# The second attention's start moved into the end of the first attention and beside its own first unit

## The chip, the cores and the metric

The kernel runs on one core of a Trainium2 chip. The metric is the device time in microseconds (us) of one execution of the whole program. Five engines work side by side, each in its own program order: TensorE (PE, matrix products and transposes), VectorE (DVE), ScalarE (ACT), GpSimd (POOL) and SyncE (SP, which here only issues DMAs). They wait for one another through semaphores.

## The reference, cut to what matters

One decoder layer in float32 on x of shape (4, 512, 256), in three stages, each followed by `x = layernorm(x + stage(x))`:

```
attention 1:  16 heads of 64, bias by relative position, softmax, output product
attention 2:  q, k, v = x @ Wq, x @ Wk, x @ Wv          (16 heads of 16, causal)
              qc = x @ Wcq;  kc, vc = ctx @ Wck, ctx @ Wcv (no mask)
              y = softmax(q k) v + softmax(qc kc) vc;  y @ Wp + bp
experts:      router picks 3 of 8 per batch; x + sum w_e * gelu(x @ Wa[e]) @ Wb[e]
```

`ctx` has shape (4, 512, 128). The layer norm after attention 1 works on each token's 256 values, so each of the four batches can be normed by itself.

## The kernel before

`x_acc` keeps x in SBUF (16 tiles of 128 tokens by 256) through the whole program. Products run on pairs of half-precision numbers (`hi` and `lo`), three matmuls for one product. `xhi` and `xlo` hold x turned, channels on the partitions.

**attention_1** goes through 32 units (8 head pairs in each of 4 batches, `u // PAIRS` is the batch) in a software pipeline of 37 slots `t`, each of four steps `i`. In slot t unit t is projected, unit t-1 has its maxima taken, t-2 and t-3 their scores and exponentials, and t-4 its output product, added to `x_acc` (`project_out` on PE, `weigh` on ACT, `add_out` on DVE and POOL). Batch 0 is complete in `x_acc` after unit 7. SP moves each unit's halves with 12 DMAs; its bias tiles `rtile` (the relative bias for the maxima) and `near` were loaded in the first eight slots by `load_bias` and kept for all 32 units. PE's own weights are split into halves by ACT (`whi`) and then DVE (`wlo`) while the first slots run, those of the output product by `split_wo` in slot 2.

An all-engine barrier follows (L636), and then **attention_2**, which before its pipeline runs a serial prologue: load ctx and the weights `w2`; norm all 16 tiles (`Normalise`: DVE statistics, ACT root, half of the tiles scaled on DVE, half on ACT); turn ctx (L760) and split it into `chi`, `clo`; split `w2` (L923, L996); turn x for all batches (`Transposed`, L104, L110, L120); and compute the values of all batches (L771 into `v`, stored at L930). Then come 16 units (4 head groups in each of 4 batches) on a clock `CLOCK` that begins at -16, 16 ticks to a unit. The engines walk through the same ticks, and each does what its tick lists:

```
CROSS, SELF, MAX, ROWS_AT, SCORE, VALUE, COPY, TURN, ADD = -12, -5, 16, 33, 38, 42, (49, 57), (56, 63), 64
```

So unit 0 has its cross projection at ticks -12 and -11, its self projection at -5 and -4, unit 1 the same 16 ticks later, and unit 0's maxima (`maximum`, L829 on PE, L1023 on DVE) take ticks 16 to 31, one unit after the other from there. A projection goes PE (L771), ACT (`high_cross` L946, `high_self` L938), DVE (`low_cross` L1012, `low_self` L1006), then SP stores the halves and, when units u and, for an even u, u+1's cross half have been stored, loads them back with 8 DMAs (L745 to L751). `maximum(0, 0)` waits for those 8. Exponentials begin at tick 38.

Afterwards come `output_2`, the router and the experts, which the change does not touch.

Of the kernel before, what the change touches and what calls it, by code (L numbers as in the profile page):

```python
# [11 lines left out]
P = 128  # L12
# [113 lines left out]
def attention_1(nc, io, x_acc, xhi, xlo, ident, lines32, lines16, far_lines):  # L126
# [5 lines left out]
    with ExitStack() as ctx:  # L132
# [3 lines left out]
        def bank(n):  # L136
            return ctx.enter_context(nc.psum_tensor(f"a1_{n}", [P, 512], F32))

        sm = semaphores(nc, ctx, "a1", "x0 x1 x2 x3 w0 w1 w2 w3 w4 w5 w6 w7 bias0 bias1 bias2 bias3 bias4 bias5 bias6 bias7 "
                                       "ld_id ld_bias st_pe st_ev st_r st_l st_f wo cst wsa wsb woa wob ones "  # L140
                                       "pe_a act_a act_v dve_a moved0 moved1 moved2 pe_b dve_b pe_rows act_rows pe_s dve_s act_s pool_p act_ps "
                                       "pool_lo pe_sum dve_r pe_o act_o dve_o pe_e0 pe_e1 dve_x act_x pool_x")
# [7 lines left out]
        rtile = sb("rtile", [P, H1, BAND], F16)  # L150
# [26 lines left out]
        turned = Transposed(nc, ctx, "t1", bank_e, x_acc, ident, (xhi, xlo))  # L177

# [9 lines left out]
        def sync(sp):  # L188
            def load_bias(pair):
                h = slice(2 * pair, 2 * pair + 2)  # L190
                sp.dma_start(rtile[:, h, :], bass.AP(lines16.tensor, 2 * pair * LINE, [[1, P], [LINE, 2], [1, BAND]])
                             ).then_inc(sm[f"bias{pair}"], DMA)
                sp.dma_start(near[:, h, :], bass.AP(lines32.tensor, 2 * pair * S + NEAR_AT, [[1, P], [S, 2], [1, REACH]])
                             ).then_inc(sm[f"bias{pair}"], DMA)
# [5 lines left out]
            def load_w(n):  # L200
                k, cut = w_cuts[n]
                sp.dma_start(wst[n], io["qkv_wT"][k * P:(k + 1) * P, cut]).then_inc(sm[f"w{n}"], DMA)
# [22 lines left out]
            load_bias(0)  # L225
            sp.wait_ge(sm["st_f"], DMA)
            for u in range(UNITS):
# [25 lines left out]
        def tensor(pe):  # L253
# [114 lines left out]

            for t in range(SLOTS):
                for i in range(NT):  # L370
# [23 lines left out]
                    if 0 <= u < UNITS:  # L394
                        pv(u, (i + 2) % 4)

        def scalar(act):
            turned.scalar(act, 0, 1)

            def split_w(n):  # L400
                k, cut = w_cuts[n]
                act.wait_ge(sm[f"w{n}"], DMA)
                act.activation(whi[:, k, cut], wst[n], ACT.Copy, scale=WS).then_inc(sm["wsa"], 1)

            def split_wo():
                act.wait_ge(sm["wo"], DMA)
                act.activation(wohi[:, :, :], wost[:, :, :], ACT.Copy, scale=WS).then_inc(sm["woa"], 1)

# [64 lines left out]
            for t in range(SLOTS):  # L473
                for i in range(NT):
# [25 lines left out]
                    if 0 <= t - 4 < UNITS:  # L500
                        weigh(t - 4, i)

        def vector(dve):
# [7 lines left out]
            def split_wo():  # L511
                dve.wait_ge(sm["woa"], 1)
                dve.scalar_tensor_tensor(wolo[:, :, :], wost[:, :, :], WS, wohi[:, :, :], ALU.mult, ALU.subtract
                                         ).then_inc(sm["wob"], 1)

# [12 lines left out]
            def maximum(u, qb):  # L528
                if qb == 0 and u > 1:
                    dve.wait_ge(sm["pe_rows"], u - 1)  # L530
                if qb == 0 and u < PAIRS:
                    dve.wait_ge(sm[f"bias{u}"], 2 * DMA)
# [1043 lines left out]
```

## Time and profile before

| | us |
|---|---|
| median of three runs (the runs) | 1340.9 (1340.89, 1340.9, 1348.62) |
| profiled execution, its own time | 1347.11 |
| its span | 1345.4 |
| PE, DVE, ACT, POOL busy | 1190.8, 913.5, 830.3, 479.5 |
| granted TensorE clock, mean | 0.951 of full |

The span is cut by the barriers: attention 1 fills it up to 556.4, attention 2 and its output product lie from there to 1048, the router to 1079, the experts to the end. Times on the trace are from the span's start. PE counts as busy while matmuls are in flight, even where they stream at the lower clock.

### The profile page before, as it was taken

How to read it: one execution, taken by the hardware profiler on the slowest of the kernel's cores; microseconds unless marked ns; L12 is line 12 of the kernel's file. 1: busy time of each engine (PE TensorE's matmuls, PEld its weight loads, DVE VectorE, ACT ScalarE, POOL GpSimd, SP SyncE). 2: the span in 40 equal slices, each digit the busy share in tenths (PEclk: the TensorE clock that was granted, in tenths of full speed). 3: DMA queues.
4: the chain of work that ended last, by engine and by line, in shares of the span. 5: the costliest groups of instructions: out<-in, count | busy, mean ns of one | idle time of the engine just before them, and what ended most of it. 6: DMA issues, size and time to landing. Idle time of an engine off the chain costs nothing. (4 is left out here: it accounts for less than half of the span.)

```text
span 1345.4 us, 25018 instructions
## 1 busy us (share of the span) xinstructions
PE 1190.8 (89%) x8862; PEld 552.4 (41%) x8862; DVE 913.5 (68%) x2337; ACT 830.3 (62%) x1584; POOL 479.5 (36%) x511
## 2 busy tenths in 40 slices
PE   6699999999999999375888888888888369999998
PEld 2244444444444443261222232232224336666666
DVE  3777777777777777435788887878841755756564
ACT  3466666666666666450577777677773465666663
POOL 0267888877888888420112111111220000000000
PEclk9999999999999999696799999999997679999999
DMA  7544222222222221202121211212100082332100
GB/s 220 156 98 103 54 57 50 49 51 57 54 57 52 49 49 24 89 8 84 46 69 49 68 52 47 68 46 60 44 2 1 2 313 78 127 125 80 64 16 17
DMA packets 75954, 91.98 MB, mean 68 GB/s; under 512 B 12242, under 2 KB 67538, under 8 KB 75798
## 3 DMA queue, kind: packets, MB, share of 16 engines
q1 hardware_dynamic: 74806, 90.25, 23.9%
q8 instruction: 71, 1.16, 0.4%
q14 instruction: 53, 0.43, 0.1%
q0 software_dynamic: 1024, 0.13, 0.1%
HBM read 54.36 MB, written 10.68 MB: 48 GB/s over the span
## 5 line engine op out<-in xcount | busy, mean ns | idle before, releaser
L1023 DVE TENSOR_REDUCE a_mx<-a_m 128x1 f32<-128x512 f32 (+3 forms) x512 | 269.0, 584 | 74.6 <-PE a_m L829 62.8
L960 ACT ACTIVATE a_pt<-a_s 128x512 f32<-128x512 f32 (+3 forms) x512 | 235.5, 515 | 88.4 <-PE a_s L857 85.1
L449 ACT ACTIVATE a_pt<-a_s 128x512 f32<-128x512 f32 x256 | 149.4, 597 | 164.3 <-DVE a_s L544 135.8
L829 PE MATMUL a_m<-a_k,a_q 48*128 48x512 f16 (+3 forms) x512 | 131.0, 362 | 53.9 <-DVE a_mx L1023 44.2
L537 DVE CUSTOM_DVE_ANT_0 a_junk<-a_m,a_rtile 128x512 f16<-128x512 f32 x256 | 167.3, 687 | 2.0 <-issue 2.0
L604 POOL TENSOR_TENSOR a_ps<-a_ps,a_pt 128x512 f32<-128x512 f32 x128 | 159.9, 1272 | 1.4 <-ACT a_pt L449 1.4
L333 PE MATMUL a_o<-a_pt,a_v 128*64 128x512 f32 x512 | 139.0, 621 | 0.1
L829 PEld LDWEIGHTS a_m<-a_k,a_q 48*128 48x128 f16 x512 | 36.2, 94 | 202.1 <-DVE a_mx L1023 160.7
L870 PE MATMUL a_o<-a_pt,a_v 128*17 128x512 f32 (+3 forms) x1024 | 119.1, 538 | 0.0
L544 DVE TENSOR_TENSOR a_s<-a_s,a_near 128x218 f32<-128x218 f32 (+1 forms) x256 | 108.0, 433 | 15.5 <-PE a_s L324 12.9
L857 PE MATMUL a_s<-a_q,a_k 49*128 49x512 f16 (+3 forms) x512 | 114.4, 352 | 3.3 <-ACT a_pt L960 3.1
L1074 POOL TENSOR_SCALAR_AFFINE_SELECT a_pt<-a_pt 128x512 f32<-128x512 f32 x64 | 40.8, 637 | 210.1 <-ACT a_pt L960 210.1
L1377 ACT ACTIVATE ex_h<-ex_up 128x512 f32<-128x512 f32 x96 | 57.4, 598 | 81.9 <-PE ex_up L1334 81.8
L323 PE MATMUL a_s<-a_q,a_k 128*128 128x512 f16 x256 | 98.9, 387 | 7.6 <-ACT a_pt L449 6.2
L616 POOL TENSOR_TENSOR x_acc<-x_acc,a_part 128x256 f32<-128x256 f32 x128 | 93.1, 727 | 35.2 <-DVE x_acc L564 31.4
L1348 PE MATMUL ex_down<-ex_whi,ex_hh 128*128 128x256 f16 x384 | 104.7, 273 | 0.1
L1348 PE MATMUL ex_down<-ex_wlo,ex_hh 128*128 128x256 f16 x384 | 104.7, 273 | 0.0
L1348 PE MATMUL ex_down<-ex_whi,ex_hl 128*128 128x256 f16 x384 | 104.7, 273 | 0.0
L526 DVE TENSOR_TENSOR a_nat<-a_a,a_nat 128x512 f16<-128x512 f32 x64 | 44.3, 692 | 84.2 <-ACT a_nat L424 84.2
L604 POOL TENSOR_TENSOR a_ps<-a_pt 128x512 f32<-128x512 f32 x64 | 80.1, 1273 | 56.3 <-ACT a_pt L449 56.3
L324 PE MATMUL a_s<-a_q,a_k 74*128 74x512 f16 x256 | 97.8, 382 | 0.0
L609 POOL TENSOR_TENSOR a_psh<-a_ps,a_psh 128x512 f16<-128x512 f32 x64 | 72.9, 1160 | 63.3 <-ACT a_psh L455 63.3
(208 smaller groups left out, 2430.8 us busy)
## 6 DMA issues: line engine op xcount, KB each, us to landing
a_q<-a_nat SPq DMA_DIRECT2D x192, 64.0 KB
a_k<-a_nat SPq DMA_DIRECT2D x192, 64.0 KB
ex_raw<-in_Wa SPq DMA_DIRECT2D x12, 1024.0 KB, 4.9
ex_raw<-in_Wb SPq DMA_DIRECT2D x12, 1024.0 KB, 7.1
halves<-a_natc SPq DMA_DIRECT2D x32, 128.0 KB, 2.4
halves<-a_nat SPq DMA_DIRECT2D x16, 256.0 KB, 2.1
a_q<-halves SPq DMA_DIRECT2D x32, 128.0 KB, 2.7
a_k<-halves SPq DMA_DIRECT2D x32, 128.0 KB, 2.8
```

The lines of the kernel that those rows point to most:

```text
L323: pe.matmul(bank_s[h][:, :], k1[c][:, h, ks], q1[c][:, h, ::-1], start=True, stop=False)
L333: mm = pe.matmul(bank_o[h * D1:(h + 1) * D1, :], v[u % 3][:, kb, h * D1:(h + 1) * D1], pt[:, (8 * u + 2 * kb + h) % RING, :], start=kb == ...
L449: act.activation(pt[:, n % RING, ::-1], bank_s[j % 2][:, :], ACT.Exp, scale=SC1 / QS).then_inc(sm["act_s"], 1)
L537: dve.tensor_tensor_reduce(junk[h][:, :], bank_m[h][:, :], rtile[:, u % PAIRS * 2 + h, qb * P:qb * P + S], 1.0, -3e38, ALU.add, ALU.max, m ...
L544: dve.tensor_tensor(bank_s[h][:, first:end], bank_s[h][:, first:end], near[:, u % PAIRS * 2 + h, at:at + end - first], ALU.add).then_inc(s ...
L604: pool.tensor_tensor(ps[h][:, :], pt[:, (8 * u + h) % RING, :] if kb == 1 else ps[h][:, :], pt[:, (8 * u + 2 * kb + h) % RING, :], ALU.add ...
L829: mm[h] = pe.matmul(bank_m[j % 3][:, 0:keys], q[u % 3][o:o + ROW_M, pair, x, qb * P:(qb + 1) * P], k[u % 3][o:o + ROW_M, pair, x, 0:keys], ...
L857: pe.matmul(bank_s[(32 * u + j) % 3][:, first:], k[u % 3][o:o + ROWS, h // 2, x, kb * P:(kb + 1) * P], q[u % 3][o:o + ROWS, h // 2, x, fir ...
L870: mm = pe.matmul(bank_o[h * 2 * D2:h * 2 * D2 + D2 + 1, first:], v[u // GROUPS][:, x * NT + kb, u % GROUPS * G2 + h, :], pt[g % 4][:, h, f ...
L960: act.activation(pt[g % 4][:, h, first:], bank_s[(32 * u + j) % 3][:, first:], ACT.Exp, scale=SC2 / QS).then_inc(sm["act_s"], 1)
L1023: dve.tensor_reduce(mx[u % 2][:, qb, to:to + 1], bank_m[j % 3][:, 0:keys], AX.X, ALU.max).then_inc(sm["dve_b"], 1)
L1348: mm = pe.matmul(down[t][:, :], a[k][:, f, tok], w[k][:, HALF + f * C:HALF + (f + 1) * C], start=i == 0, stop=i == len(steps) - 1)
```

## The change

Three things are moved.

1. The second attention's weights, small constants and context are loaded during the first. `w2` is split in slots 6 and 10 (`split_w2`, 1280 columns each) out of the buffer `wost`, ctx is turned and split in slot 35 (`turn_context`, `high_context`, `low_context`). To make room, `rtile` becomes a ring of three tiles, reloaded for each unit (`load_toeplitz`, 32 loads in place of 8).
2. Batch 0 is normed (statistics in slot 34, the rest in slot 35) and turned (slot 36) inside attention 1.
3. Batches 1 to 3 are normed, turned, and all values computed, at ticks of attention 2's own clock, in the banks of the scores: statistics at ticks -2, 2, 6; turns at 5 and 6, 12 and 13, 18 and 19; values of batch 0 at -11, -10, -5, -4, of batch 1 at 7, 8, 9, 11, of batch 2 at 14 to 17, of batch 3 at 21, 23, 25, 27.

```diff
+class LayerNorm:           # as Normalise, for one batch b (done: how many were normed before)
+    def statistics(self, dve, b, done):   # 4 bn_stats, 4 bn_aggr, + EPS
+    def root(self, act, b, done):         # Sqrt
+    def even(self, dve, b, done):         # reciprocal, shift, 2 tensor_scalar on x_acc
+    def odd(self, act, b, done):          # 2 activations on x_acc
...
 def attention_1
+            def load_toeplitz(u):
+                if u >= 3:
+                    sp.wait_ge(sm["dve_b"], 8 * (u - 3) + 8)
+                sp.dma_start(rtile[:, u % 3, :, :], bass.AP(lines16.tensor, 2 * (u % PAIRS) * LINE, [[1, P], [LINE, 2], [1, BAND]])
+                             ).then_inc(sm[f"rt{u % 3}"], DMA)
...
+                if u + 1 < UNITS:
+                    load_toeplitz(u + 1)
                 if u + 1 < PAIRS:
-                    load_bias(u + 1)
+                    load_near(u + 1)
+                if u == 4:    # tri_q, identm, ident16, b2, then the first half of w2 into wost
...
+                if u == 8:    # second half of w2
...
+                if u == 12:   # ctx
...
         def tensor(pe):
+                    if t == SLOTS - 2:
+                        turn_context(i)
+                    if t == SLOTS - 1 and i < KC:
+                        turn_first(i)
...
         def scalar(act):
+                    if t in (6, 10) and i == 1:
+                        split_w2(t // 10)
+                    if t == SLOTS - 2:
+                        high_context(i)
+                        if i == 0:
+                            norm.root(act, 0, 0)
+                        if i == 1:
+                            norm.odd(act, 0, 0)
+                    if t == SLOTS - 1 and i < KC:
+                        high_first(i)
...
         def vector(dve):
+                    if t in (6, 10) and i == 1:
+                        split_w2(t // 10)
...
+                    if t == SLOTS - 3 and i == NT - 1:
+                        norm.statistics(dve, 0, 0)
+                    if t == SLOTS - 2:
+                        if i == 1:
+                            norm.even(dve, 0, 0)
+                        low_context(i)
+                    if t == SLOTS - 1 and i < KC:
+                        low_first(i)
...
 def attention_2
+        NORM, TURN_X = (None, -2, 2, 6), (None, (5, 6), (12, 13), (18, 19))
+        VALUES = (-11, -10, -5, -4), (7, 8, 9, 11), (14, 15, 16, 17), (21, 23, 25, 27)
...
         def tensor(pe):
-            (ctx turned, all batches turned, all values)
+            def free(n):       # a bank of the ring bank_s: its last tenant read by ACT (and DVE)
+            def turn_x(b, k):
+                n = turn_number(b, k)
+                free(n)
+                norm.ready(pe, b + 1)
+                for t in range(NT):
+                    o = (b * NT + t) * C + k * P
+                    mm = pe.transpose(bank_s[n % 3][:, t * P:(t + 1) * P], x_acc[:, o:o + P], ident[:, :])
+                mm.then_inc(sm["pe_f"], 1)
+            def values(b, i):
+                n = value_number(b, i)
+                free(n)
+                pe.wait_ge(sm["dve_f"], 2 * b)
...
                 for b in range(B):                 # in each tick after maximum and score,
+                    if b > 0 and n in TURN_X[b]:   # before the projections
+                        turn_x(b, TURN_X[b].index(n))
+                    if n in VALUES[b]:
+                        values(b, VALUES[b].index(n))
...
         def scalar(act):
+                for b in range(1, B):              # in each tick ahead of rows, high_self, high_cross
+                    if n == NORM[b] + 1:
+                        norm.root(act, b, b)
+                    if n == NORM[b] + 2:
+                        norm.odd(act, b, b)
+                (high_x and store_values at the ticks of TURN_X and VALUES)
...
         def vector(dve):
+                for b in range(1, B):              # in each tick ahead of low_self, low_cross
+                    if n == NORM[b]:
+                        norm.statistics(dve, b, b)
+                    if n == NORM[b] + 2:
+                        norm.even(dve, b, b)
+                    if n in TURN_X[b]:
+                        low_x(b, TURN_X[b].index(n))
```

## Rows read from the trace of the kernel before

**Rows 1.** The page's 40 equal slices: granted clock of PE in tenths

```profile
PEclk9999999999999999696799999999997679999999
```

**Rows 2.** Windows: length, busy us of each engine (instructions), clock, DMA share, GB/s

```profile
557.00:582.00 25.00, 10.66 (x48) 9.39 (x48) 20.17 (x58) 13.73 (x24) 0.97 (x5) 0.59 0.38 119
582.00:598.60 16.60, 15.88 (x144) 14.02 (x144) 0.00 (x0) 9.53 (x16) 9.23 (x4) 1.00 0.00 1
598.60:617.30 18.70, 5.26 (x23) 1.76 (x25) 3.00 (x4) 2.79 (x5) 0.00 (x0) 0.85 0.34 98
617.30:640.00 22.70, 18.16 (x82) 5.25 (x82) 18.02 (x34) 1.38 (x2) 0.00 (x0) 0.65 0.20 59
```

**Rows 3.** DVE's timeline in attention 1's full slots, a reciprocal per slot (start, us)

```profile
78.30 0.21 DVE L556 RECIPROCAL a_r<-a_e 128x8 f32<-128x8 f32 x1 [0.42 <-PE a_e L348]
...
140.53 0.21 DVE L556 RECIPROCAL a_r<-a_e 128x8 f32<-128x8 f32 x1 [0.42 <-PE a_e L348]
...
342.63 0.21 DVE L556 RECIPROCAL a_r<-a_e 128x8 f32<-128x8 f32 x1 [0.42 <-PE a_e L348]
```

**Rows 4.** Timeline around `split_wo` in slot 2

```profile
53.12 1.91 ACT L407 ACTIVATE a_wohi<-a_wost 128x2048 f16<-128x2048 f32 x1
...
55.07 2.29 DVE L513 SCALAR_TENSOR_TENSOR a_wolo<-a_wost,a_wohi 128x2048 f16<-128x2048 f32 x1 [1.11 <-ACT a_wohi L407]
...
58.50 0.39 PE L323 MATMUL a_s<-a_q,a_k 128*128 128x512 f16 x1 [2.97 <-ACT a_pt L449]
```

**Rows 5.** Timeline of attention 1's last slots

```profile
547.28 0.48 DVE L564 SCALAR_TENSOR_TENSOR x_acc<-a_e,a_r,x_acc 128x256 f32<-128x256 f32 x1 [3.96 <-PE a_e L365]
...
549.43 0.40 PE L365 MATMUL a_e<-a_wohi,a_a 64*128 64x256 f16 x2 [0.35 <-issue]
...
550.26 0.48 DVE L564 SCALAR_TENSOR_TENSOR x_acc<-a_e,a_r,x_acc 128x256 f32<-128x256 f32 x1 [0.93 <-PE a_e L365]
...
551.75 0.48 DVE L564 SCALAR_TENSOR_TENSOR x_acc<-a_e,a_r,x_acc 128x256 f32<-128x256 f32 x1 [1.00 <-PE a_e L365]
```

**Rows 6.** Timeline of attention 2's prologue

```profile
556.41 5.32 DVE L59 BATCH_NORM_STATS2 t_st<-x_acc 128x6 f32<-128x256 f32 x16 [1.21 <-PEq L636]
...
561.66 1.15 DVE L62 BATCH_NORM_AGGREGATE t_mv<-t_st 128x2 f32<-128x6 f32 x16
...
563.16 1.97 PE L760 MATMUL a_m<-ident,a_pt 128*128 128x128 f32 x8 [8.45 <-DMA a_pt<-in_ctx]
...
563.67 2.67 DVE L70 TENSOR_SCALAR x_acc<-x_acc,t_mv,t_rs 128x256 f32<-128x256 f32 x8
563.79 4.04 ACT L78 ACTIVATE x_acc<-x_acc,t_rs 128x256 f32<-128x256 f32 x8 [0.53 <-DVE t_rs L68]
...
577.86 0.60 ACT L110 ACTIVATE xhi<-a_s 128x512 f16<-128x512 f32 x1 [1.89 <-PE a_s L104]
578.15 0.68 DVE L120 TENSOR_TENSOR xlo<-a_a,xhi 128x512 f16<-128x512 f32 x1
```

**Rows 7.** Timeline: ACT's change of tables before the first exponentials

```profile
646.16 1.28 ACT L960 ACT_TABLE_LOAD   x1
...
647.60 2.06 ACT L960 ACTIVATE a_pt<-a_s 128x512 f32<-128x512 f32 x4 [0.16 <-PE a_s L857]
```

**Rows 8.** Timeline from unit 0's self projection to its first maximum

```profile
604.03 0.75 DVE L1006 SCALAR_TENSOR_TENSOR a_nat<-a_a,a_bias,a_nat 128x512 f16<-128x512 f32 x1 [2.28 <-ACT a_nat L938]
...
606.42 0.75 DVE L1012 SCALAR_TENSOR_TENSOR a_natc<-a_a,a_bias,a_natc 128x512 f16<-128x512 f32 x1 [1.64 <-ACT a_natc L946]
...
617.27 0.29 PE L829 MATMUL a_m<-a_k,a_q 48*128 48x128 f16 x2 [8.57 <-DMA a_k<-halves]
```

**Rows 9.** Windows of 4 us, columns as in Rows 2

```profile
612.00:616.00 4.00, 0.00 (x0) 0.00 (x0) 0.00 (x0) 0.00 (x0) 0.00 (x0) 0.50 0.64 184
...
632.00:636.00 4.00, 3.96 (x15) 0.74 (x13) 2.17 (x4) 0.69 (x1) 0.00 (x0) 0.53 0.01 2
```

**Rows 10.** Timeline: DVE behind a projection placed between unit 0's maxima

```profile
623.54 1.29 DVE L1023 TENSOR_REDUCE a_mx<-a_m 128x1 f32<-128x512 f32 x2 [1.27 <-PE a_m L829]
```

More of the change, by code:

```diff
@@ new lines, with __init__ @@
+QK_AT, CQ_AT, CK_AT = 0, KC * GROUPS * P, KC * GROUPS * P + KC * C
+V_AT = CK_AT + C
+W2 = V_AT + (KC + 1) * C
+class Second:
+    def __init__(self, nc, ctx, x_acc):
+        self.norm = LayerNorm(nc, ctx, "n1", x_acc)
+        self.whi, self.wlo, self.tri_q, self.identm, self.ident16, self.chi, self.clo = (
+            ctx.enter_context(nc.sbuf_tensor(f"a2_{n}", shape, F16))
+            for n, shape in (("whi", [P, W2]), ("wlo", [P, W2]), ("tri_q", [P, 2, P]), ("identm", [P, 2, P]),
+                             ("ident16", [P, P]), ("chi", [P, B * S]), ("clo", [P, B * S])))
+        self.braw, self.bias = (ctx.enter_context(nc.sbuf_tensor(f"a2_{n}", [P, 2 * GROUPS], F32)) for n in ("braw", "bias"))
@@ L132, in attention_1 @@
+def attention_1(nc, io, x_acc, xhi, xlo, ident, second, lines32, lines16, far_lines):
     with ExitStack() as ctx:
@@ L177, in attention_1 @@
         turned = Transposed(nc, ctx, "t1", bank_e, x_acc, ident, (xhi, xlo))
+        norm = second.norm
+        W2_CUTS = [slice(i * (W2 // 2), (i + 1) * (W2 // 2)) for i in range(2)]
+        w2_raw = wost[:, :, :].rearrange("p a c -> p (a c)")[:, 0:W2 // 2]
+        craw = wost[:, :, :].rearrange("p a (t c) -> p (a t) c", c=CC)
+        bank_c = [*bank_s, *bank_m]
+        bank_x = [bank_a, bank_s[0]]
         UNITS = PAIRS * B
@@ L367, in project_out, with turn_context, turn_first @@
                             mm.then_inc(sm[f"pe_e{h}"], 1)
+            def turn_context(b):
+                pe.wait_ge(sm["act_s"], 8 * UNITS)
+                pe.wait_ge(sm["dve_b"], 8 * UNITS)
+                pe.wait_ge(sm["ld_ctx"], DMA)
+                for n in range(NT):
+                    mm = pe.transpose(bank_c[b][:, n * P:(n + 1) * P], craw[:, b * NT + n, :], ident[:, :])
+                mm.then_inc(sm["pe_c"], 1)
+            def turn_first(k):
+                norm.ready(pe, 1)
+                pe.wait_ge(sm["act_rows"], 2 * UNITS)
+                pe.wait_ge(sm["dve_c"], 1)
+                for n in range(NT):
+                    mm = pe.transpose(bank_x[k][:, n * P:(n + 1) * P], x_acc[:, n * C + k * P:n * C + (k + 1) * P], ident[:, :])
+                mm.then_inc(sm["pe_x"], 1)
             for t in range(SLOTS):
@@ L530, in maximum @@
                     dve.wait_ge(sm["pe_rows"], u - 1)
-                if qb == 0 and u < PAIRS:
-                    dve.wait_ge(sm[f"bias{u}"], 2 * DMA)
+                if qb == 0:
+                    dve.wait_ge(sm[f"rt{u % 3}"], DMA * (u // 3 + 1))
                 for h in range(2):
@@ L542, in add_bias @@
                 first, end, at = near_columns(kb)
+                if j == 0 and u < PAIRS:
+                    dve.wait_ge(sm[f"near{u % 2}"], DMA * (u // 2 + 1))
                 dve.wait_ge(sm["pe_s"], 8 * u + j + 1)
@@ L672, in attention_2 @@
         bank_a, bank_o = bank("a"), bank("o")
-        flat = [t[:, :, :].rearrange("p a b -> p (a b)") for t in pt]
-        craw = flat[2].rearrange("p (t c) -> p t c", c=CC)
-        raw = [flat[i][:, 0:W2 // 2] for i in range(2)]
-        w_cuts = [slice(i * (W2 // 2), (i + 1) * (W2 // 2)) for i in range(2)]
-        norm = Normalise(nc, ctx, "t2", x_acc)
-        turned = Transposed(nc, ctx, "t2", bank_s + [bank_a], x_acc, ident, (xhi, xlo))
-        bank_v = bank_m + [bank_a]
+        norm = second.norm
         UNITS = GROUPS * B
@@ L977, in scalar @@
                     exponential(u, 2 * i + 1)
+                for b in range(1, B):
[3 more added lines that the diff above has]
+                        norm.odd(act, b, b)
+                for b in range(B):
+                    if b > 0 and n in TURN_X[b]:
+                        high_x(b, TURN_X[b].index(n))
+                    if n in VALUES[b]:
+                        store_values(b, VALUES[b].index(n))
                 u, i = unit_at(n, ROWS_AT)
```

215 lines of the change are left out of this document (128 added, 87 removed).

## The prediction

> **What bounds the kernel now.** I read the page's slices first: PE's granted clock is at its upper level almost everywhere and falls in two places, slices 17 to 20 and 31 to 33 [rows 1]. The chain that ended last is no help for the first of them, since it is followed back only as far as the experts' first load. So I cut the stretch around the first dip into windows [rows 2]. From 557.0 to 582.0 PE works 10.66 of 25.0 us: norm, loads, weight splits, turns. From 582.0 to 598.6 it computes all values, dense and alone (DVE does nothing). From 598.6 to 617.3 it works 5.26 of 18.7: four projections with their hand-overs, the stores, the loads back. So 60.9 us pass from the barrier (DVE's first instruction at 556.41 [rows 6]) to the first maximum at 617.27 [rows 8]; in them only the values need PE. This is what the change attacks. The stretches on both sides are full. In attention 1 a slot takes 15.55 us ((140.53 - 78.30) / 4 and (342.63 - 140.53) / 13 both give it [rows 3]), one behind the other without a gap. In attention 2's first unit DVE is busy 18.02 of 22.7 us and PE 18.16, at a mean clock of 0.65 [rows 2]: what is put there is not free.
>
> **Part 1, the loads in attention 1.** Twenty-four more loads of `rtile` (448 KB each) stand in SP's queue behind the twelve moves of their slot. In the four slots from 78.30, three of which still issue a bias load (and `near` with it), a slot takes the same 15.55 us as in the thirteen after, which issue none [rows 3]. So I take 0 for them. The wait on `dve_b` that each has is for the maxima of two slots back, and is over when SP comes to it. Two `split_w2` stand in ACT's and DVE's order at step 1 of slots 6 and 10. The row nearest to them is `split_wo`: 1.91 us on ACT and then 2.29 on DVE for 2048 columns, after which PE stood still for 2.97 us [rows 4], 1.2 less than the two together. Scaled to 1280 columns the two take 1.2 + 1.4 = 2.6 us; less the same 1.2 of slack PE loses 1.4. Two of them: **2.8 us** (0 if the slack is wider in the full slots, 5.2 if there is none).
>
> **Part 2, the end of attention 1.** Prices: statistics of one batch (5.32 + 1.15) / 4 and a small sum, 1.8; four turns by PE 1.0 (half of 1.97); a half on ACT 0.60 and on DVE 0.68; two tiles scaled on DVE 0.67 and on ACT 1.0 [rows 6]; a change of tables 1.28 [rows 7]. Statistics begin on DVE at 547.76, behind the last add of slot 34 [rows 5], and end at 549.57, so the reciprocal of slot 35 and its output product start 0.45 later, at 549.85. Before, a round of slot 35 (product 0.83, add 0.48, hand-overs) took 1.49 [rows 5]. Now each round has a context turn on PE, a half on ACT, a half on DVE. Round 0: product to 550.7, turn to 551.75, ACT's half to 552.35, tables to 553.6, root to 553.85. ACT's `weigh` of round 1, which before would have begun at once, begins then. DVE waits for the root too, scales (to 555.0) and splits; ACT scales to 556.0. Round 2's product is done by 555.4 but is weighed only at 556.0 to 556.45; round 3's product runs to 557.5, its turn to 558.5, batch 0's two turns to 560.6, and the last half on DVE ends at 562.0. The barrier falls at about 562.35 in place of 556.41: **5.9 us** later (4 to 8: the tables hidden, or everything in a row).
>
> By the Trainium skill ("ScalarE: Activation LUTs", What ACT_TABLE_LOAD costs) a switch takes about 2.66 us with its drain. Here ACT was back 0.16 us after the load's 1.28, and that 0.16 was for PE [rows 7]; by the page the sum below would be 1.2 us poorer. The number of switches is the same before and after.
>
> **Part 3, from the barrier to the first maximum.** At the upper clock a product of 512 columns takes 0.22 us per matmul and the values 16.6 / 144 = 0.11 [rows 2]. PE: cross(0) first half, `values(0,0)` 1.3, cross(0) second half, done at 565.2. ACT stores those values first (0.6) and then does `high_cross`; DVE's half is done at 566.8. The self projection with the other values of batch 0 between runs to 569.1, and DVE's `low_self(0)` ends at 570.65: 8.3 after the barrier. Before, this took 6.2 (598.6 to 604.78 [rows 2, 8]), so the values cost 2.1 there.
>
> Now comes the wait that the change adds. Before, `low_cross(1)` ended at 607.17, 2.4 after `low_self(0)` [rows 8], and SP needs it before it loads unit 0 back. Now DVE has in front of it: statistics(1), even(1), statistics(2), even(2), low_x(1,0), low_x(1,1), statistics(3). By the prices above, with ACT's roots between (0.5 each with hand-overs): 1.8 + 0.3 + 1.15 + 1.8 + 0.3 + 1.15 = 6.5, at 577.1. ACT scales batch 2 until 577.45, then `high_x(1,0)`, then `high_cross(1)`, then `high_x(1,1)` to 579.35; DVE's second low_x ends at 580.1, statistics(3) at 581.9, `low_cross(1)` at **582.65**: 12.0 after `low_self(0)` in place of 2.4. From there to the first maximum nothing changes: 617.27 - 607.17 = 10.1 [rows 8]. First maximum at 592.75. PE meanwhile does values(1), self(1), turns of batch 2 and two of its values, and by its terms is done at 591.6, just in time. So the front takes 30.4 in place of 60.9. With part 2, the first maximum comes **24.5 us** earlier.
>
> **Part 4, unit 0's maxima.** Still to be done between them on PE: two values of 0.65, two turns of 1.0, batch 3's values (1.3, 1.3, 0.65, 0.65); on DVE two low_x. Half a projection (three matmuls of 0.43 at the lower clock) there left DVE idle for 1.27 [rows 10], so the bank ring of three hides little of it; the same half at the upper clock, 0.65, I take as hidden, and of anything longer 0.6. At the upper clock: turns (1.0 and ACT's 0.6 less what DVE has queued, 0.6; then 0.69 of DVE) 2 x 1.3; long values 2 x 0.7; short ones near 0; in all 4.6. The four projection halves there, 1.3 each before, get 0.65 shorter at the upper clock and give back about 2. Net **2.6**. At the lower clock throughout it is 10.7 (long values 2.6 us each, short 1.3).
>
> **The clock.** PE stood idle for 8.57 us up to 617.27 [rows 8] and its clock was at 0.50 in the window 612 to 616; it was 0.53 still in 632 to 636, with PE busy 3.96 of 4 [rows 9]. In the new order PE's first long idle stretches are 571.5 to 574.3 and 576.4 to 580.1; before and after them it is denser than it was. Each of the three places (batch 0's values and projections, 6.5 us of streams; batch 1's and 2's, 8; the first unit) would run part of its time at 1.2 GHz. Price if all of it does: 5 before `low_self(0)`, 4 before the first maximum, 8 in the unit (10.7 less 2.6). I take a quarter of these 17: **4 us**. This share is a choice; its ends are 0 and 17.
>
> **Sum.** 24.5 - 2.8 - 2.6 - 4 = **15 us**. On the profiled execution 1347.1 would become 1332; the median of the runs lies 6 us under it for reasons outside this stretch, and I carry the same difference over: **1326**.
>
> **The rivals.**
> 1. *The fillers and splits are hidden*: the ring and the slack absorb parts 1 and 4, the clock is up. 24.5 - 0 - 0.5 - 0 = 24: 1317. For it: PE idles in front of the maxima for DVE. Against it: rows 4 and 10.
> 2. *The lower clock stays* from the barrier (mean 0.59 from 557 to 582 [rows 2]) through the first unit: 24.5 - 2.8 - 2.6 - 17 = 2: 1339, no change. Against it: in the first dense stretch after that, from 582.0, the clock was 1.00 at once, and the new front has the same values in it. The skill ("TensorE: Matmul & The Clock Gate", What's actually happening) says that the throttled state is the default and activity releases it; by that this rival ends where the values begin.
> 3. *Slower*: the `rtile` stream is not free. It decides from 15 / 24 = 0.63 us per slot; if each load keeps the moves behind it back so that a slot takes 1.5 us more, 36 us are lost in 24 slots and the time is 1341 + 21 = 1362. For it: these loads now go on in slots where SP's next moves follow closely. Against it: the equal slots [rows 3].
> 4. *It doesn't shorten the front as told*: the norms' chain is longer than my 12.0 (each hand-over 0.2 more, roots behind table loads, 3 x 1.28). Gain 15 - 7 = 8: 1333.
>
> **How the numbers follow.** Forecast (gain 10 to 20) 0.55, hidden 0.15, lower clock 0.13, longer chain 0.11, slower 0.06. The range goes from 1316 to 1338, down to rival 1 and up nearly to rival 2. A difference under 1% (13.4 us) can hardly be told from none here. The bound lies at 1327.5, near my number: of the forecast's 0.55 about 0.42 lies beyond it, with rival 1 0.57, and some of the chain's, so 0.6 faster, 0.33 the same, 0.07 slower.
>
> **What would show it.** Slots of 15.55 us in attention 1 except for two that are about 1.4 longer; the second attention's first instruction near 565 on the new trace (562.35 and the 2.8); `low_cross(1)` some 12 us behind `low_self(0)`, with norm instructions between; the first maximum 30 to 34 us after the barrier; a first unit of 25 to 29 us; no row changed behind it. I am wrong if the slots are longer, if the clock's 0.50 reaches through the first unit, or if PE, not the loads back, releases the first maximum by many us.

## The result and the profile after

The changed kernel takes **1323.46 us** (median of four runs, 1322.84 to 1324.3) where the kernel before, run beside it, takes 1341.38 (1340.89 to 1348.62). The ratio is 0.9854, with a 95% interval from 0.982 to 0.9888: 17.9 us between the medians, 1.5% by the ratio. The forecast was 1326 with a range from 1316 to 1338. The profiled execution took 1322.84 with a span of 1321.1.

First the page of the changed kernel, as in [rows 1]: in slices 17 to 20 the granted clock reads 8, 8, 8, 7 in place of 6, 9, 6, 7, and the load of `rtile` is there 32 times.

```profile
PEclk9999999999999999888799999999999689999999
...
a_rtile<-lines SPq DMA_DIRECT2D x32, 448.0 KB, 3.9
```

Next DVE's timeline of the changed kernel in attention 1, as in [rows 3]: a slot takes 15.55 us as before (127.55 to 143.09, 223.00 to 238.55) with a tile loaded in each of them, but 17.71 from 109.84 to 127.55, where the first half of `w2` is split. The second such slot, 174.19 to 191.89, takes 17.70.

```profile
109.84 0.21 DVE L707 RECIPROCAL a_r<-a_e 128x8 f32<-128x8 f32 x1 [0.42 <-PE a_e L441]
127.55 0.21 DVE L707 RECIPROCAL a_r<-a_e 128x8 f32<-128x8 f32 x1 [0.43 <-PE a_e L441]
143.09 0.21 DVE L707 RECIPROCAL a_r<-a_e 128x8 f32<-128x8 f32 x1 [0.42 <-PE a_e L441]
...
223.00 0.21 DVE L707 RECIPROCAL a_r<-a_e 128x8 f32<-128x8 f32 x1 [0.43 <-PE a_e L441]
238.55 0.21 DVE L707 RECIPROCAL a_r<-a_e 128x8 f32<-128x8 f32 x1 [0.42 <-PE a_e L441]
```

The timeline inside that slot (start, length, engine, operation, and in brackets the idle time before it and what ended it), to be held against [rows 4]. ACT works 1.27 us, DVE 1.58, and PE then stands for 1.24 because `a_a` comes from DVE, which was busy with the split. Nine of the profiles of this study have two such slots; sixteen of the eighteen take 17.7 and two take 19.1 and 19.2 (norms later, tail). In these two PE stands for the same 1.24, but the granted clock is down to 0.66 and 0.75 in the 4 us that follow, where the changed kernel has 1.00.

```profile
116.12 1.27 ACT L524 ACTIVATE a_whi<-a_wost 128x1280 f16<-128x1280 f32 x1
...
117.43 1.58 DVE L653 SCALAR_TENSOR_TENSOR a_wlo<-a_wost,a_whi 128x1280 f16<-128x1280 f32 x1 [0.64 <-ACT a_whi L524]
...
119.75 1.08 PE L426 MATMUL a_o<-a_pt,a_v 128*64 128x512 f32 x4 [1.24 <-DVE a_a L700]
```

The timeline of attention 1's end in the changed kernel, as in [rows 5]. The statistics stand in front of slot 35's reciprocal; then the change of tables, the root 0.02 us behind it, the scaling between the adds; the last `xlo`; and attention 2's first instructions, POOL's at 566.22 and PE's at 566.26 (before, DVE's at 556.41 [rows 6]).

```profile
552.72 1.39 DVE L140 BATCH_NORM_STATS2 n_st<-x_acc 128x6 f32<-128x256 f32 x4
...
554.52 0.19 DVE L707 RECIPROCAL a_r<-a_e 128x8 f32<-128x8 f32 x1
...
557.33 1.28 ACT L150 ACT_TABLE_LOAD   x1
...
558.63 0.20 ACT L150 ACTIVATE n_rs<-n_rs 128x4 f32<-128x4 f32 x1
...
565.25 0.68 DVE L663 TENSOR_TENSOR xlo<-a_s,xhi 128x512 f16<-128x512 f32 x1
...
566.22 1.08 POOL L1239 MEMSET a_v<- 128x128 f32 x3 [2.39 <-POOLq L800]
...
566.26 0.38 PE L914 MATMUL a_a<-xhi,a_whi 128*128 128x512 f16 x1 [1.84 <-PEq L800]
```

The timeline of the new front, as in [rows 8]: `low_self(0)`, then three rounds of statistics, and only then `low_cross(1)` at 585.74. SP's first load back is issued at 589.57, and the first maximum is at 597.71 after an idle of 1.50 in place of 8.57.

```profile
573.70 0.75 DVE L1177 SCALAR_TENSOR_TENSOR a_nat<-a_a,a_bias,a_nat 128x512 f16<-128x512 f32 x1 [3.16 <-ACT a_nat L1106]
...
577.45 1.40 DVE L140 BATCH_NORM_STATS2 n_st<-x_acc 128x6 f32<-128x256 f32 x4
...
583.29 1.40 DVE L140 BATCH_NORM_STATS2 n_st<-x_acc 128x6 f32<-128x256 f32 x4
...
585.74 0.74 DVE L1183 SCALAR_TENSOR_TENSOR a_natc<-a_a,a_bias,a_natc 128x512 f16<-128x512 f32 x1
...
589.57 0.61 SPq L901 DMA_DIRECT2D a_q<-halves  x1
...
597.71 0.23 PE L990 MATMUL a_m<-a_k,a_q 48*128 48x128 f16 x2 [1.50 <-DMA a_k<-halves]
```

Windows of the changed kernel, columns as in [rows 2]: barrier to first maximum, the first three units, and the stretch from the last unit's maxima to the router.

```profile
566.20:597.00 30.80, 20.48 (x133) 14.65 (x133) 14.87 (x48) 14.48 (x27) 8.48 (x8) 0.83 0.23 65
...
597.71:620.53 22.82, 19.24 (x138) 9.53 (x138) 19.05 (x36) 6.16 (x10) 2.35 (x1) 0.95 0.21 60
...
620.50:643.10 22.60, 19.72 (x123) 6.25 (x123) 18.45 (x35) 11.43 (x24) 3.75 (x6) 0.65 0.21 59
643.10:668.70 25.60, 23.73 (x190) 7.21 (x192) 18.95 (x39) 17.18 (x37) 3.58 (x6) 0.88 0.18 53
...
971.89:1024.41 52.52, 42.22 (x262) 23.36 (x254) 9.03 (x19) 27.52 (x57) 5.78 (x9) 0.97 0.00 1
```

The last one in the kernel before:

```profile
990.07:1048.60 58.53, 49.05 (x262) 24.01 (x254) 9.03 (x19) 27.74 (x57) 5.78 (x9) 0.83 0.00 1
```

To measure a unit I use DVE's small operation that closes its maxima (the first maximum opens the first). Of these closings the kernel before has, for units 0, 1, 2 and 15,

```profile
640.02 0.18 DVE L1030 TENSOR_SCALAR a_mx<-a_mx 128x32 f16<-128x32 f32 x1
...
663.23 0.18 DVE L1030 TENSOR_SCALAR a_mx<-a_mx 128x32 f16<-128x32 f32 x1
...
686.88 0.18 DVE L1030 TENSOR_SCALAR a_mx<-a_mx 128x32 f16<-128x32 f32 x1
...
990.07 0.18 DVE L1030 TENSOR_SCALAR a_mx<-a_mx 128x32 f16<-128x32 f32 x1
```

and the changed kernel

```profile
620.53 0.18 DVE L1201 TENSOR_SCALAR a_mx<-a_mx 128x32 f16<-128x32 f32 x1
...
643.14 0.18 DVE L1201 TENSOR_SCALAR a_mx<-a_mx 128x32 f16<-128x32 f32 x1
...
668.70 0.18 DVE L1201 TENSOR_SCALAR a_mx<-a_mx 128x32 f16<-128x32 f32 x1
...
971.89 0.18 DVE L1201 TENSOR_SCALAR a_mx<-a_mx 128x32 f16<-128x32 f32 x1
```

So the account of the two profiled executions is:

| stretch | before, us | after, us | earlier by |
|---|---|---|---|
| start to attention 2's first instruction | 556.41 | 566.22 | -9.8 |
| from there to the first maximum | 60.9 | 31.5 | +29.4 |
| unit 0's maxima | 22.75 | 22.82 | -0.1 |
| units 1 and 2 | 46.86 | 48.17 | -1.3 |
| units 3 to 15 | 303.2 | 303.2 | 0 |
| from there to the router | 58.5 | 52.5 | +6.0 |

At the end of the maxima the changed kernel is 18.2 us ahead, which is what the medians say (17.9). The 6.0 in the last line are a stretch at the lower clock (0.83 against 0.97 in the windows above) in which nothing was changed; the first experiment asks whether they belong to the kernel.

### The profile page after: what moved, and what is told of

Read it like the earlier page. It is cut to its first block and busy times, and to the rows that moved or that the text cites. A ratio compares the mean times of both kernels' runs of the same rounds, so it can differ in the third digit from the quotient of the medians.

```text
span 1321.1 us, 25115 instructions
## 1 busy us (share of the span) xinstructions
PE 1182.4 (89%) x8862; PEld 549.9 (42%) x8862; DVE 915.6 (69%) x2346; ACT 830.9 (63%) x1587; POOL 479.5 (36%) x511
## 5 line engine op out<-in xcount | busy, mean ns | idle before, releaser
L1038 PE MATMUL a_o<-a_pt,a_v 128*17 128x512 f32 (+3 forms) x1024 | 116.4, 527 | 0.0
```

The source lines that it names most:

```text
L1038: mm = pe.matmul(bank_o[h * 2 * D2:h * 2 * D2 + D2 + 1, first:], v[u // GROUPS][:, x * NT + kb, u % GROUPS * G2 + h, :], pt[g % 4][:, h, f ...
```

## The experiments

My theory was the prediction's: the gain comes from laying norms, turns and values beside the projections, and what limits it is a chain on DVE up to `low_cross(1)` and the loads behind it. Against it stood that the hoisted loads bring it, that another queue limits the new front, and that the fillers and splits cost either nothing or their full length.

### The kernel before, once more

Nothing is edited.

> The kernel before, unchanged, traced a second time. The two traces differ by 24.3 us in span, but only 18.2 of it is there when the last unit's maxima end (990.1 before, 971.9 changed); the other 6 us lie between there and the router, where the trace of before shows a granted clock of 0.50 from 1004 to 1020 and that of the changed kernel does not. Theory A: this is an accident of that one execution, no effect of the change; this trace has its span near 1339 and the clock at 1.00 in the second attention's last units, as the two runs at 1340.9 suggest. Theory B: the old order brings it about; the span is near 1345 again with the same low stretch.

It took 1339.01, the median of 13 runs of the same kernel on that chip being 1342.9 (1339.05 to 1347.75). Its first maximum is at 616.25 and the last unit closes at 988.22, 372.0 apart (372.8 in the first profile). The last stretch has 52.35 us at a clock of 0.97:

```profile
988.22:1040.57 52.35, 42.05 (x262) 23.23 (x254) 9.04 (x19) 27.43 (x57) 5.79 (x9) 0.97 0.01 1
```

So the 6 us are of one execution. In all thirteen profiles of this study, this stretch took 52.35 to 52.8 in nine and 56.4 to 58.5 in four, kernels before and changed among both. Attention 1 moves from one execution to the next as well: its first reciprocal is at 77.2 to 79.7 in the thirteen. So a place on one trace held against the same place on another is good to a us or two; lengths between near marks are firmer.

### Norms later in the front

```diff
-        NORM, TURN_X = (None, -2, 2, 6), ...
+        NORM, TURN_X = (None, -2, 7, 9), ...
```

> The changed kernel with the norms of batches 2 and 3 moved from ticks 2 and 6 to ticks 7 and 9, behind low_cross(1). Theory A (VectorE's queue in front of low_cross(1) sets the loads back of unit 0 and so the first maximum): low_cross(1) ends about 8 us behind low_self(0) in place of 12.0, and the loads are back 4 us earlier. TensorE's values of batch 2 then become what is late, about 2 us before the old first maximum, so 1321 to 1322. Theory B (TensorE's fillers, not the loads, set the first maximum): no change, 1323.5.

Measured 1322.65 (1319.55 to 1326.03), ratio 0.9853 [0.9813, 0.9893]: no gain over the change. In the timeline `low_cross(1)` starts 7.9 us after `low_self(0)` (574.16 to 582.05) in place of 12.0, and the loads back are issued 3.7 earlier. Yet the first maximum is at 598.56, and nothing stands idle before it:

```profile
582.05 0.74 DVE L1183 SCALAR_TENSOR_TENSOR a_natc<-a_a,a_bias,a_natc 128x512 f16<-128x512 f32 x1
...
585.89 0.60 SPq L901 DMA_DIRECT2D a_q<-halves  x1
...
594.18 0.27 PE L914 MATMUL a_s<-a_whi,xhi 128*128 128x256 f16 x1 [2.85 <-DVE xlo L1173]
...
598.56 0.23 PE L990 MATMUL a_m<-a_k,a_q 48*128 48x128 f16 x2
```

PE waited 2.85 for batch 2's `xlo`, which the later norm had delayed, and then had its values in the queue ahead of the maximum. PE's own queue is a second limit, close behind the first: in the changed kernel PE had stood idle for only 1.50 before its first maximum. The prediction had put PE's end at 591.6 and the loads at 592.75.

### Everything ahead of the projections

```diff
-        CLOCK = range(-SLOT, ...)
-        NORM, TURN_X = (None, -2, 2, 6), (None, (5, 6), (12, 13), (18, 19))
-        VALUES = (-11, -10, -5, -4), (7, 8, 9, 11), (14, 15, 16, 17), (21, 23, 25, 27)
+        CLOCK = range(-4 * SLOT, ...)
+        NORM, TURN_X = (None, -60, -57, -54), (None, (-51, -50), (-45, -44), (-39, -38))
+        VALUES = (-55, -54, -53, -52), (-49, -48, -47, -46), (-43, -42, -41, -40), (-37, -36, -35, -34)
```

> The changed kernel with all norms, turns and values of the second attention placed at ticks -60 to -34, ahead of the first projection: only the loads, the splits, the context and batch 0's norm and turn stay in the first attention, and nothing lies beside the hand-overs or unit 0's maxima. This parts the gain in two. Theory A: the interleaving carries most of it. The serial part takes about 10 us of norms and turns and 16.5 of values, then 6.1 to low_self(0) and 12.5 to the first maximum, 45 in place of 31.5, so 1337. Theory B: the hoisted loads carry it and the interleaving is only hidden work in another place: under 1328.

Measured 1343.03 (ten runs, 1338.78 to 1348.1), ratio 1.0002 [0.9984, 1.002]. Windows of this kernel: barrier to first maximum, and unit 0.

```profile
565.18:618.18 53.00, 28.74 (x190) 20.35 (x191) 17.58 (x50) 18.64 (x35) 10.95 (x9) 0.82 0.15 43
618.18:640.86 22.68, 18.00 (x82) 5.27 (x82) 18.02 (x34) 1.37 (x2) 0.00 (x0) 0.65 0.20 59
```

The hoisted part shortens the front by 7.9 us, from 60.9 to 53.0, and attention 1 ends at 565.18 in place of 556.41, 8.8 later, so alone it is worth nothing. The interleaving, put on top of it, takes the front from 53.0 to 31.5 and carries the whole gain. (Interleaving without the hoisting was not tried.) My expectation had 45 us for this front and was 8 too short; the clock was at 0.50 from 576 to 584, and where the rest of the 8 lies was not followed. Unit 0 takes 22.7 with nothing but projections between its maxima, at a clock of 0.65.

### The context and batch 0 a slot earlier

```diff
-                    if t == SLOTS - 2:
+                    if t == SLOTS - 3:
                         turn_context(i)
-                    if t == SLOTS - 1 and i < KC:
+                    if t == SLOTS - 2 and i < KC:
                         turn_first(i)
...
-                    if t == SLOTS - 3 and i == NT - 1:
+                    if t == SLOTS - 3 and i == 0:
                         norm.statistics(dve, 0, 0)
```

with ACT's and DVE's parts moved likewise.

> The changed kernel with the context turned and split in slot 34 in place of 35, batch 0's norm there too, and its turn in slot 35 in place of 36. Theory A (the last slots are longer by 5 us because these steps stand between the rounds of the output product, while slot 34 has idle stretches of some 4 us on TensorE, ScalarE and VectorE, waiting for GpSimd's sums): the barrier comes 3 to 4 us earlier, 1319.5 to 1320.5. Theory B (the steps delay GpSimd's chain in slot 34 by as much as they free in slot 35): within 1 us of 1323.5.

Measured 1323.51 (1320.58 to 1327.55), ratio 0.987 [0.9833, 0.9907]. From slot 34's reciprocal on (543.42 here, 543.07 in the change) the end of attention 1 is 2.1 us shorter, 21.1 in place of 23.2. But `low_self(0)` starts at 573.74, where the change has 573.70: from attention 2's first product to it are 9.2 us in place of 7.4. PE has the lower clock in 564 to 568, the changed kernel 1.00 there.

```profile
564.00:568.00 4.00, 3.46 (x14) 2.05 (x15) 0.48 (x1) 0.00 (x0) 1.48 (x5) 0.50 0.13 27
```

It is tempting to lay this at the new order: before its barrier PE is busy 1.82 of the 4 us from 560 to 564, in the change 3.86 of 4. The other profiles don't bear that out. The lighter front, the light and the heavy kernel below leave the instructions up to `low_self(0)` as they are in the change, and they too take 8.7 to 9.1 us for the stretch, with the clock down. This is the heavy one's; the change has the same 48 matmuls in 7.44 us, at 1.00.

```profile
564.93:574.04 9.11, 8.35 (x48) 5.29 (x48) 1.24 (x2) 3.77 (x6) 3.76 (x6) 0.81 0.28 75
```

Both profiles of the change, norms later, pieces and fill take 7.4. So what took the 2.1 back is slower matmuls behind the barrier; that the new order brings this about is not shown. The four times of the whole kernel, 1320.58 to 1327.55, show neither a gain nor a loss.

### A lighter front

```diff
-        NORM, TURN_X = (None, -2, 2, 6), (None, (5, 6), (12, 13), (18, 19))
-        VALUES = ..., (7, 8, 9, 11), (14, 15, 16, 17), (21, 23, 25, 27)
+        NORM, TURN_X = (None, -2, 7, 11), (None, (7, 8), (14, 15), (22, 23))
+        VALUES = ..., (9, 10, 11, 12), (17, 18, 19, 21), (24, 26, 28, 29)
```

> The changed kernel with norms 2 and 3 at ticks 7 and 11, batch 1's turn at 7 and 8 (behind both halves of the cross projection of unit 1) and its values at 9 to 12, and all of batch 2's values moved behind the first maximum (ticks 17 to 21, turn at 14 and 15), batch 3's at 24 to 29. e2_norms_later brought the loads back 4 us earlier and gained nothing, because TensorE had batch 2's values, at the lower clock, in its order in front of the first maximum. Theory A (two queues hold the first maximum: VectorE's in front of low_cross(1), TensorE's fillers in front of the maximum): low_cross(1) ends some 5.5 us behind low_self(0), the first maximum some 17 in place of 23.3, and unit 0's slot grows by 1 to 3: 1318.5 to 1320.5. Theory B (what is moved into the slot is paid there in full): within 1 us of 1323.5.

Measured 1323.97 (1323.52 to 1324.3), ratio 0.9863 [0.9832, 0.9894]. `low_cross(1)` now comes 4.9 us after `low_self(0)`, the first maximum at 592.41, 5.3 earlier (4.2 if both are counted from attention 2's first product). Timeline and window:

```profile
578.85 0.75 DVE L1183 SCALAR_TENSOR_TENSOR a_natc<-a_a,a_bias,a_natc 128x512 f16<-128x512 f32 x1 [1.08 <-ACT a_natc L1114]
...
592.41 0.23 PE L990 MATMUL a_m<-a_k,a_q 48*128 48x128 f16 x2
```

```profile
592.41:622.79 30.38, 23.23 (x163) 12.66 (x162) 21.21 (x39) 9.21 (x16) 4.69 (x2) 0.88 0.17 53
```

Unit 0 takes 30.4 in place of 22.8: 25 more matmuls, 2.2 us more of DVE, and 0.88 for 0.95 of clock. What leaves the front is paid in the unit with interest: it closes 2.3 later than in the change (622.79 to 620.53). Units 1 and 2 then take 47.06 in place of 48.17, and the last unit closes at 972.29, within 0.4 of the change.

### The weight split in eight pieces

```diff
-                    if t in (6, 10) and i == 1:
-                        split_w2(t // 10)                  # 1280 columns
+                    if t in (6, 7, 10, 11) and i in (1, 3):
+                        split_w2((6, 7, 10, 11).index(t) * 2 + i // 2)     # 320 columns
```

> The changed kernel with the split of the second attention's weights cut into eight pieces of 320 columns, at steps 1 and 3 of slots 6, 7, 10 and 11, in place of two of 1280. In the changed kernel each of the two lengthens its slot from 15.55 to 17.70. Theory A (a slot has a slack of about 0.7 us on VectorE and ScalarE, which is 2.85 of work less 2.15 of delay, at each place): a piece costs 0.34 + 0.4 us and is hidden, no slot is longer than 15.6, 1319.2. Theory B (no slack, the delay is proportional to the work): the four slots are each longer by 1.1, 1323.5.

Measured 1323.79 (1321.03 to 1325.92), ratio 0.9858 [0.9824, 0.9893]. DVE's reciprocals of this kernel:

```profile
108.99 0.21 DVE L710 RECIPROCAL a_r<-a_e 128x8 f32<-128x8 f32 x1 [0.42 <-PE a_e L444]
125.48 0.19 DVE L710 RECIPROCAL a_r<-a_e 128x8 f32<-128x8 f32 x1
142.38 0.19 DVE L710 RECIPROCAL a_r<-a_e 128x8 f32<-128x8 f32 x1
158.35 0.21 DVE L710 RECIPROCAL a_r<-a_e 128x8 f32<-128x8 f32 x1 [0.42 <-PE a_e L444]
```

From 108.99 to 158.35 are 49.36 for three slots, 2.7 more than 3 x 15.55, for one half of `w2`; the other half, from 173.89 to 223.83, costs 3.3. The change pays 2.15 for each. Small pieces hide no better than big ones: the slack of 0.7 us at each place that my first theory took is not there.

### TensorE kept busy in unit 0

Fourteen matmuls of 512 columns into a bank that nobody reads then are added, one in each tick from 28 to 41.

```diff
+                if 28 <= n < 42:
+                    pe.matmul(bank_o[:, :], whi[:, 0:P], xhi[:, 0, 0:S], start=True, stop=True)
```

> The changed kernel with 14 more matmuls of 512 columns, one per tick from 28 to 41, written to the output bank, where unit 0's values later start anew. They compute nothing that is used. The granted clock of the changed kernel is 1.00 through most of unit 0's maxima and falls to 0.50 from about 618 to 636, where TensorE is less busy, and again at 644. Theory A (the pause of TensorE's work at the end of unit 0's maxima lets the clock fall, and work there holds it up): 1.00 from 600 on, unit 1's maxima shorter than 22.6 and unit 2's 23.65 in place of 25.6, in all 1 to 3 us earlier. Theory B (the clock is not what these slots wait for, VectorE is): the clock is up, the marks stay within 0.5 us, or the slot gets longer by the added matmuls.

Measured 1323.36 (1319.09 to 1324.74), ratio 0.9852 [0.9816, 0.9889]. Windows of it:

```profile
620.00:624.00 4.00, 4.00 (x21) 1.19 (x20) 3.16 (x8) 0.59 (x1) 1.20 (x2) 0.50 0.01 2
624.00:628.00 4.00, 4.00 (x18) 1.23 (x17) 2.30 (x6) 2.41 (x3) 0.00 (x0) 0.58 0.00 0
628.00:632.00 4.00, 3.80 (x28) 1.42 (x25) 4.00 (x9) 3.37 (x8) 0.79 (x2) 1.00 0.27 66
```

The clock is up from 628 on, where the changed kernel has 0.50 in 628 to 632 and again in 644 to 648; over unit 1 it is 0.81, and 0.64 to 0.67 in the same unit of the nine other interleaved profiles. That the fill raises the clock is seen. That it gains time is not: unit 1 takes 22.35, and norms later has 22.29 at 0.67. Unit 2 takes 23.65 for the change's 25.56, but so it does in three interleaved kernels without a fill. Units 3 to 15 take 303.9 here, 302.4 to 303.2 elsewhere. The median shows no gain either. The first four of the added matmuls stand between unit 0's last maxima, which take 22.9 in place of 22.8: there some 0.9 us of work (4 x 0.22) was nearly free.

### Tail, front and pieces together

The edits of the three experiments on them in one kernel.

> e4_tail, e5_front and e6_pieces together. e4_tail brought the barrier about 2 us earlier (beside the same marks in slot 34) and lost it in the first projections, which ran at the lower clock. If the parts add: 4 from the pieces, 4 from the front, 0 to 2 from the tail, 1314 to 1316. If the first maximum's queue takes in what comes earlier, as it did in e4_tail, 1319.

Measured 1325.29 (1323.39 to 1331.7), ratio 0.9887 [0.9846, 0.9929]. The first maximum is at 592.38, unit 0 closes at 622.85, the last unit at 972.41, 0.5 behind the change. My expectation was 1314 to 1319: the parts don't add, since the lighter front pays its gain back in unit 0 (30.5 us), the pieces cost more than the two splits, and what the tail gains is gone before `low_self(0)`. No version beats the change.

### Lighter and heavier values in unit 0

In the first, batch 3's four values have 12 matmuls in place of 36; in the second 72.

```diff
-                steps = [... for s in ((wh, xh), (wl, xh), (wh, xl))]
-                    mm = product(bank_s[n % 3][:, t * C:(t + 1) * C], parts)
+                steps = [... for s in ((wh, xh), (wl, xh), (wh, xl))][::every]
+                    mm = product(bank_s[n % 3][:, t * C:(t + 1) * C], parts, every=3 if b == 3 else 1)
```

```diff
+                    for again in range(2 if b == 3 else 1):
                         mm = product(bank_s[n % 3][:, t * C:(t + 1) * C], parts)
```

> The four values of batch 3 stand between the first unit's maxima with 12 matmuls in place of 36 (the low halves' products are left out for that batch, so its values are less exact). In the changed kernel that unit takes 22.8 us at a mean clock of 0.95, as long as without any values in it at 0.65 (22.7 before). Theory A (the values are not free; the upper clock that they go with has paid for them): 24 matmuls of 256 columns are 2.6 us at the upper clock. If the clock stays up, the unit takes 20.3 to 21.5; if it falls with the work gone, it is back at 22 to 23. Either way the clock and the time go together. Theory B (the values fill idle time of TensorE and cost nothing at any clock): 22.8 whatever the clock, and 22.8 at a clock of 0.95 as well. Whole kernel: A 1321.5 to 1323.5, B 1323.5.

> Each product of batch 3's four values is done twice, one behind the other with the same result: 36 more matmuls of 256 columns between the first unit's maxima, 3.9 us at the upper clock. Theory A (not free): the unit takes 25.5 to 27 in place of 22.8, and the kernel 1326 to 1328. Theory B (they fill idle time; TensorE is busy 19.24 of 23.5 us there, so 4.3 us are empty): 22.8 to 23.5, kernel 1323.5 to 1324.

Measured 1324.44 (1321.21 to 1327.1), ratio 0.9859 [0.9834, 0.9883], and 1328.19 (1327.66 to 1328.72), ratio 0.9896 [0.9875, 0.9916]. Unit 0 in the first, and in the second:

```profile
600.00:622.98 22.98, 18.41 (x114) 7.53 (x114) 18.99 (x37) 6.15 (x10) 2.35 (x1) 0.89 0.20 59
```

```profile
597.84:624.58 26.74, 22.61 (x174) 12.98 (x174) 19.08 (x36) 6.15 (x10) 2.35 (x1) 0.97 0.18 50
```

The lighter unit runs from its first maximum at 600.25 to 622.98, 22.7 us: 24 matmuls fewer and not faster, with the clock at 0.89. It is at 1.00 up to 612 and 0.83, 0.75 and 0.68 in the three windows of 4 us after that. The heavier takes 3.9 us more than the change, the full length of its 36 matmuls at the upper clock (36 x 0.11 = 3.9), though PE had 3.6 us idle there. With the clock already up, this work costs all of its time. In the light kernel the first eight matmuls less bring the unit forward by 0.9, their full length; behind them the clock falls, and the last two projection halves, at 0.43 us a matmul in place of 0.22, take it back. The fill, in short pieces between the last maxima, is the exception. My expectation for the heavy one was 25.5 to 27, that for the light one let both ways open.

### The changed kernel, once more

Nothing is edited.

> The changed kernel once more, nothing altered. It shows which low-clock stretches of the first profile of it belong to the kernel and which don't. In that profile unit 2's maxima took 25.6 us with a clock of 0.50 at 644 to 648, where three variants had 23.65. Theory A (that stretch is of one execution only): unit 2 takes 23.65 here and the stretches elsewhere lie in other places. Theory B (it belongs to the kernel): 25.6 again. Time 1323.5, within 2.

Measured 1324.1 (1323.06 to 1325.86), ratio 0.9861 [0.9841, 0.9882]. Unit 0 takes 22.81 at a clock of 0.97, and units 1 and 2

```profile
619.30:642.29 22.99, 20.14 (x123) 6.19 (x123) 18.44 (x35) 11.43 (x24) 3.73 (x6) 0.65 0.20 58
642.29:667.70 25.41, 23.63 (x190) 7.27 (x192) 18.94 (x37) 17.18 (x37) 3.57 (x6) 0.87 0.19 53
```

so unit 2's longer time is not of one execution, as I had believed: that theory fell. It is 25.4 to 27.0 in five of the ten profiles of interleaved orders (the change twice, norms later, pieces, heavy), 24.3 in the light one and 23.65 in the other four (tail, lighter front, fill, and the three together). In both profiles of the kernel before and in the serial front it is 23.65. What decides between the two is open; the clock over unit 2 is 0.82 to 0.94 in the six where it is long and 1.00 in the seven where it takes 23.65. To the end of the last unit's maxima, this profile is 18.05 us ahead of the second profile of the kernel before (970.17 to 988.22), as the first pair was 18.2. The last stretch took 57.0 at 0.85 here, and 52.5 at 0.97 in the first profile: that one does change from execution to execution.

## Why the prediction was right

The forecast was 15 us, the measured gain 17.9, and the mechanism is the one predicted. By its steps:

- **`rtile` stream, 0.** Right: slots of 15.55 with a load in each. The slower rival (from 0.63 us a slot) is refuted, and so is the longer chain, rival 4, by the 12.0 below.
- **Two splits, 2.8.** Mis-sized: 4.3, 2.15 each. I had subtracted the 1.2 us of slack that [rows 4] show while the pipeline still fills. A full slot has less: of 1.27 + 1.58, the slot loses 2.15, and in eight pieces more. The 5.2 that the prediction gave as its upper end was a little nearer than the value taken.
- **End of attention 1, 5.9.** Measured 5.0 to 5.1, by what is left of the 9.8 after the splits (4.3) and 0.4 in the start, which is of the execution and not of the change. The order was as told: statistics ahead of the reciprocal, the table load before the root and before `weigh` of round 1. The Trainium skill's rule ("ScalarE: Activation LUTs", What ACT_TABLE_LOAD costs: about 2.66 us in all) would add 1.4, an estimate from that figure less the load's 1.28; the trace disagrees, with the root at 558.63, 0.02 after a load of 1.28 that began at 557.33.
- **Barrier to first maximum, 30.4.** Measured 31.5. `low_self(0)` ended 8.2 after the barrier (8.3 forecast) and `low_cross(1)` 12.0 after that (12.0 forecast). The missing 1.1 lies behind: SP issues the first load 3.09 us after `low_cross(1)` in both kernels, but from there to the first maximum it takes 8.14 us, where it took 7.0. The sum of [rows 8] was carried over unchanged; the six other profiles that keep the change's norms and values up to there have 7.7 to 8.1. The idle that ended there was a wait for `a_k` by DMA, so it is the loads that took longer; why is open. PE was done with its values just in time, as told, and the norms-later experiment shows how near that second limit is.
- **Unit 0, 2.6.** Measured 0.1, and the range of 25 to 29 us for it was wrong. Two parts of it were mis-sized together. The work in it is not hidden (the heavy kernel pays it in full, the lighter front too), but the clock was at 0.95 in place of 0.65, with PE denser, and the saving on the old matmuls made up for the new ones. I had 4.6 for the new and gave back 2; the light and the serial kernel, both near 22.7 at 0.89 and 0.65, say that what is given back is about as much as the new work costs. That this comes out so nearly even is luck, not something the prediction knew. One price in the 4.6 was read wrongly, too: a turn of 1.0 us comes from [rows 6] at 563.16, where the granted clock was 0.50, and was used for the upper clock; in unit 0 the two turns take 0.66 each. Rival 1 gave the right number here for a wrong reason.
- **The clock, 4.** The term was a choice. What goes with the clock is 1.3 in units 1 and 2. In the front batch 1's values from 583.5 ran at the lower level (one started every 0.21 us, 0.11 at the upper), which did not delay the first maximum, since PE still stood idle for 1.50 before it. The upper level came back in the middle of them, at 587.5, after 4 us in which PE was busy 3.98; the Trainium skill ("TensorE: Matmul & The Clock Gate", What's actually happening) says that the throttled state is the default and activity releases it, and the trace agrees. Rival 2, the low clock throughout, is refuted by 0.83 and 0.95 in the windows. The part that I priced at 5 before `low_self(0)` did not come in the changed kernel's two profiles, where the stretch from the first product takes 7.4; in five of the ten interleaved ones 1.3 to 1.8 us of it came. So how much of this term a single execution shows is chance.
- **The 6 us beside the stretch.** Carried over from the profile to the median, and right: they are of single executions, in a stretch behind all that was changed.

Put together: to the first maximum 24.5 - 2.8 = 21.7 was forecast and 19.6 measured (1.5 more for the splits, 0.4 in the start, 1.1 more in the front, 0.9 less at the end of attention 1). Behind it I had 6.6 for unit and clock, and 1.4 was lost. Splits and front were a little worse, unit and clock clearly better, and 15 became 18.2. That the total is within 3 us of the forecast is in part luck, since 2.1 too much before the first maximum stands against 5.2 too little behind it.

## What to carry to other kernels

Moving a prologue's loads, splits and first norm into the phase before was worth nothing here, since they made that phase longer (8.8 us) by as much as the prologue became shorter (7.9); what paid was to lay the prologue's arithmetic beside the waits of the next phase. Count each thing put between the critical engine's work at its full length, and then ask separately what its density does to the clock: where the clock was low, filling it in can be free. When one limit is shortened and nothing comes of it, look at the instruction ahead of the released one in its own queue.

## What the runs showed of the hardware

- In unit 0, filled time and clock traded off nearly to zero up to some 140 matmuls: it took 22.7 us with 82 matmuls at 0.65, 22.7 with 114 at 0.89, 22.8 with 138 at 0.95, 22.9 with 143 at 0.97, and 26.7 with 174 at 0.97. The lighter front, with more of VectorE's work in it too, took 30.4 with 163 at 0.88.
- The same order of instructions ran at either level from one execution to the next: from the second attention's first product to `low_self(0)` five profiles took 7.4 us at a granted clock of 1.00, and in three with the same instructions there it took 8.7 to 9.1 at a mean of 0.81 to 0.85.
- A stretch that no kernel here altered, from the last maxima to the router, took 52.35 to 52.8 us at a clock of 0.94 to 0.97 or 56.4 to 58.5 at 0.83 to 0.88, from one execution to the next. That is a third of the gain under study, so a single profile's total is no measure of it.
- Four transposes of 128x128 in float32 took 1.11 us at the lower clock (557.37) and 0.60 where it had risen to the upper (563.82).
